# Attention-times-values with the values as weights in four column tiles, in a two-layer transformer kernel on one core

## The chip, the core and the metric

The kernel runs on one core of one Trainium2 chip. Five engines work side by side: TensorE (PE: matrix products, with its weight loads, PEld, shown apart), VectorE (DVE), ScalarE (ACT), GpSimd (POOL) and SyncE (SP, which here only issues DMAs). They wait for each other through semaphores. The metric is device time in microseconds (us), the median of three runs.

## The reference, cut to what matters

The reference is a chain of four residual blocks over x of 8 batches x 100 rows x 512. The change touches the third, a quantized cross-attention with 16 heads of 32:

```python
x = x + _L0_xattn_ref(_layernorm(x), ctx, ...)
x = x + _L0_ffn_ref(_layernorm(x), ...)
x = x + _L1_xattn_ref(_layernorm(x), ctx, mask, wq, bq, wk, bk, wv, bv, wo, bo)
x = x + _L1_ffn_ref(_layernorm(x), ...)

# _L1_xattn_ref, in words: q = w8a8(x), k, v = linear(ctx)      (361 context rows)
# p = softmax(q k^T / sqrt(32) + mask)                          (100 x 361 per head)
# o = p v                                                       (100 x 32 per head)
# out = w8a8(o, wo) + bo      (o is quantized by its row: max, scale, round)
```

The core of the change is `o = p v` and the division of the softmax by its row sums.

## The kernel before, in words

The program has three stages. Stage A (up to about 300 us) makes the first two blocks and, for each batch, the keys (into `CT`) and the values (into `VS`). Stage B (about 300 to 618 us) is the attention. Stage C is the mixture of experts. All fp32 matmuls appear in the trace as two instructions each (two passes of weights); the products on `float32r` tiles (scores) and the turns (transposes) are one instruction each.

Stage B takes the eight batches one after another (`batches`, a first batch, a loop of three times two, a last one), each with 16 steps, one per head. Every engine's order is written out by hand in its own `body`; the step number is `h_`. At a step,

- PE makes the scores of head `h_` (L793, `ps` bank 0 or 1), turns the exponentials of head `h_ - 2` in three pieces of 121 context rows (L802, `TURN = 2`), and multiplies head `h_ - 3` with the values (L814, `MIX = 3`): the turned exponentials `pT` (121 x 100) are the weights, and 33 columns of `VS` are streamed, 32 values and a column of ones whose product is the row sum. Three pieces are added up in a part of bank 4 or 5.
- DVE adds the mask, negates, and takes the row minimum (L1174).
- ACT makes the exponential (L612) and copies the turned exponentials of head `h_ - 2` out of PSUM (L621).

Two buffers of each (`score`, `masked`, `exp`, `p_turned`, `p_copied`, indexed by `h_ % 2`) let the engines run at most two heads apart. Around the heads lie, at fixed steps, the works of the next batch (on DVE `prep_at`: norm, quantization and bias of the queries; on PE the turn of `xq2b` at step 5 and `queries` at step 7; on ACT `high_keys` at step 5; on POOL `low_keys`) and of the batch before (on DVE `finish_at`: `finish1` divides by the row sums at step 2, `finish2` adds a bias at 5, `finish3` finds the scale at 6, `finish4` rounds at 7, `finish5` at 13; on PE the turn of `oQb` at step 9 and `out_rows`, L783, at step 11). SP's queue restacks keys and queries for the next batch (L335): for each quarter of the heads it waits until the scores of the current batch have read it; the third quarter's keys go ahead of the queries of the first quarter. It also loads expert weights, the second half after `o_norm` (`finish1`).

Of the kernel before, what the change touches and what calls it, by code (L numbers as in the profile page):

```python
# [5 lines left out]
ALU = mybir.AluOpType  # L6
# [9 lines left out]
T = 361  # L16
P = 128
# [6 lines left out]
VW = HEADS * (HD + 1)  # L24
# [14 lines left out]
def block_kernel(nc, x, ctxT, mask, decay, win, b_in, wout, b_out, gamma0, beta0, w1, w2, gammaf,  # L39
                 wq, bq, wk, bk, wv, bv, wo, bo, gate_w, gate_b, gate_bias, ew1, eb1, ew2, out):  # L40
    with ExitStack() as whole:
# [5 lines left out]
        def sem(name):  # L47
            if name not in sems:
# [6 lines left out]
                    "o_norm", "summ_used", "t1", "t2", "v_copied", "v_mm", "x1", "x2", "x3", "y_out0", "y_out1",  # L55
                    *(f"{name}{r}" for name in ("exp", "masked", "p_copied", "p_turned", "pv", "score")
# [77 lines left out]
        pT = sb(bb, "pT", [P, 2, NT, S])  # L134
# [107 lines left out]
        TURN, MIX = 2, 3  # L242
# [150 lines left out]
        def _(g):  # L393
# [45 lines left out]
            def body(b, last):  # L439

                alone(g, ("h_round", b + 1), ("t2", after(b * 2)))
                g.tensor_scalar(hq[0:S, FF // 2:], h[0:S, FF // 2:], -MAGIC, 1.0, ALU.add, ALU.mult)\
                 .then_inc(sem("hq1"), 1)
                if not last:
                    norms(b + 1)

                g.wait_ge(sem("v_copied"), after((b + 1) * NT))
                g.tensor_copy(vs(b)[0:TC, :].rearrange("p (c h w) -> p c h w", c=NT, h=HEADS)[:, :, :, HD],
                              ones[0:TC, 0:NT * HEADS].rearrange("p (c h) -> p c h", c=NT))\
                 .then_inc(sem("v_ones"), 1)  # L450

# [4 lines left out]
            g.wait_ge(sem("v_ones"), B)  # L456
# [64 lines left out]
        def _(act):  # L521
# [84 lines left out]
            def body(b, j, u, first, last):  # L606
                for h_ in range(HEADS + (TURN if last else 0)):
                    if h_ < HEADS:
                        r, n = h_ % 2, b * 8 + h_ // 2
                        act.wait_ge(sem(f"masked{r}"), after(n + 1))  # L610
                        act.wait_ge(sem(f"p_turned{r}"), after(n))
                        act.activation(pE[0:S, r, 0:T], sN[0:S, r, 0:T], ACT.Exp, scale=-1.0,  # L612
                                       bias=nmx[0:S, h_:h_ + 1]).then_inc(sem(f"exp{r}"), 1)
                    at_turn = behind(b, h_ - TURN, first)
                    if at_turn:

                        bt, ht = at_turn
# [3 lines left out]
                        act.copy(pT[0:TC, r].rearrange("p c s -> p (c s)"), ps[0:TC, 2 + r, 0:NT * S])\  # L621
# [5 lines left out]
                    if h_ == 10 and not first:  # L627
                        turned_o(b - 1)

# [3 lines left out]
            batches(act, body)  # L633
            turned_o(B - 1)
# [28 lines left out]
        def _(pe):  # L663
            for name in credited:
                pe.sem_inc(sem(name), 1)
            pe.wait_ge(sem("consts"), 1)
# [118 lines left out]

            def body(b, j, u, first, last):
                for h_ in range(HEADS + (MIX if last else 0)):
# [18 lines left out]
                    if at_mix:  # L806
                        bm, hh = at_mix
                        r, n, hd = hh % 2, bm * 8 + hh // 2, head(hh)[2]
                        pe.wait_ge(sem(f"p_copied{r}"), after(n + 1))
                        if hh == 0:  # L810
                            pe.wait_ge(sem("o_norm"), after(bm))
# [15 lines left out]
                    if h_ == 9 and not first:  # L827
# [4 lines left out]
                    if h_ == 11 and not first:  # L832
# [7 lines left out]
            batches(pe, body)  # L840
# [70 lines left out]
        def _(dve):  # L911
# [113 lines left out]
            def body(b, last):  # L1025
# [22 lines left out]
                for c in range(NT):  # L1048
                    if c == NT - 1 and not last:
                        rows(b + 1)  # L1050
                    dve.wait_ge(sem("v_mm"), after(b * NT + c + 1))
                    dve.tensor_copy(vs(b)[0:TC, c * VW:(c + 1) * VW].rearrange("p (h w) -> p h w", h=HEADS)[:, :, 0:HD],
                                    ps[0:TC, c % 2, :].rearrange("p (h w) -> p h w", h=HEADS))\
                       .then_inc(sem("v_copied"), 1)
# [83 lines left out]
            def finish1(b):  # L1138
                chf.turn(b)
                for r in range(2):  # L1140
                    dve.wait_ge(sem(f"pv{r}"), after((b + 1) * 8))
                o = ps[0:S, 4:6, 0:8 * (HD + 1)].rearrange("p g (h w) -> p g h w", h=8)
                chf(dve.reciprocal(rinv[0:S].rearrange("p (g h) -> p g h", g=2), o[:, :, :, HD]))
                dve.tensor_tensor(oN[0:S].rearrange("p (g h w) -> p g h w", g=2, h=8), o[:, :, :, 0:HD],
                                  rinv[0:S].rearrange("p (g h) -> p g h", g=2).unsqueeze(3)
                                  .to_broadcast([S, 2, 8, HD]), ALU.mult).then_inc(sem("o_norm"), 1)

            def finish2(b):
# [3 lines left out]
            def finish3(b):  # L1152
                row_scale(chf, oN[0:S], tb[0:S, 6:7], tb[0:S, 7:8], tb[0:S, 8:9])

            def finish4(b):
# [3 lines left out]
            def finish5(b):  # L1159
# [7 lines left out]
            def body(b, j, u, first, last):  # L1167
                dve.wait_ge(sem(f"mask_in{j}"), 16 * u + 16)
                for h_ in range(HEADS + 1):
# [7 lines left out]
                    if not first and h_ in finish_at:  # L1177
                        finish_at[h_](b - 1)
# [6 lines left out]
            finish_at = {2: finish1, 5: finish2, 6: finish3, 7: finish4, 13: finish5}  # L1185
# [10 lines left out]
            for step in finish_at.values():  # L1196
                step(B - 1)
# [152 lines left out]
```

## Time and profile before

| | us |
|---|---|
| median of 3 runs (lowest to highest) | 867.86 (866.38 to 868.89) |
| span of the profiled execution | 862.6 |
| what the median has beyond that span (start and end around it) | 5.3 |
| PE busy / PE weight loads busy | 632.2 / 511.1 |
| DVE / ACT / POOL busy | 411.9 / 295.8 / 139.9 |
| six batches of stage B, from the first score of the second batch (369.54) to that of the eighth (574.79) | 205.25 |

The span is from the first to the last instruction. Busy time is a union, so a weight load that lies under a product counts in both PE rows. "Granted clock" is the share of 2.4 GHz that TensorE had; it has two levels, 0.5 (1.2 GHz) and 1.0 (2.4 GHz). A batch's pitch is the time from its first score product to that of the next batch.

### The profile page before, as it was taken

The numbers are of one execution on the slowest core, as the hardware profiler recorded it, in microseconds if no ns is written. First come the engines' busy times: TensorE is split into PE (matmuls) and PEld (weight loads), VectorE is DVE, ScalarE is ACT, GpSimd is POOL, SyncE is SP. The second block draws the span as 40 slices with busy tenths as digits, with TensorE's granted clock in tenths as the row PEclk, the third lists the DMA queues.
The fourth block names the chain that finished last, engine by engine and source line by source line (L and its number), as shares of the span: only waits on it lengthen the run. The fifth ranks groups of instructions, "written<-read, shape, count | busy, mean of one in ns | idle before, by whom it ended". The sixth has DMA issues, their size and how long they took to land.

```text
span 862.6 us, 11350 instructions
## 1 busy us (share of the span) xinstructions
PE 632.2 (73%) x3228; PEld 511.1 (59%) x3229; DVE 411.9 (48%) x972; ACT 295.8 (34%) x503; POOL 139.9 (16%) x179
## 2 busy tenths in 40 slices
PE   0145599999999813999999999999327059999920
PEld 0124377777777512998998989989227035555510
DVE  6466467666667454464655656644241112111114
ACT  4166233344443241544453444544101012222210
POOL 1001133222133001210111101200000600000044
PEclk9985699999999955555555555555555579999975
DMA  8968000000000126537446465471300422222135
GB/s 350 370 238 262 10 10 9 9 9 0 9 9 1 32 87 134 108 109 169 113 121 143 114 148 122 115 165 68 88 14 0 126 87 85 85 85 85 61 83 169
DMA packets 57158, 86.42 MB, mean 100 GB/s; under 512 B 19858, under 2 KB 43186, under 8 KB 55114
## 3 DMA queue, kind: packets, MB, share of 16 engines
q1 hardware_dynamic: 54062, 79.57, 31.4%
q0 software_dynamic: 3072, 6.56, 2.8%
q8 instruction: 11, 0.18, 0.1%
q14 instruction: 13, 0.11, 0.0%
HBM read 47.88 MB, written 15.42 MB: 73 GB/s over the span
## 4 chain that ended last, share of the span: by engine, by line
PE 43%; DVE 5%; issue 4%; DMA 4%; POOL 3%; ACT 2%; SPq 1%; POOLq 0%; DVEq 0%; ACTq 0%
PE ps L814 12%; PE ps L802 7%; PE ps L901 7%; PE ps L887 6%; PE ps L793 5%; DMA b1B<-in_eb 1%; PE ps L783 1%; POOL picked L515 1%; PE ps L776 1%; POOL slots_in L508 1%; PE ps L861 1%; ACT hTe L648 1%; DMA q<-qH 1%; PE ps L893 1%; PE ps L855 1%
## 5 line engine op out<-in xcount | busy, mean ns | idle before, releaser
L814 PEld LDWEIGHTS ps<-VS,pT 121*100 121x100 f32 x768 | 132.7, 268 | 14.6 <-issue 12.3
L814 PE MATMUL ps<-VS,pT 121*100 (+1 forms) x768 | 134.6, 329 | 9.1 <-ACT pT L621 6.5
L612 ACT ACTIVATE pE<-sN,nmx 100x361 f32<-100x361 f32 x128 | 76.4, 598 | 145.4 <-DVE nmx L1174 145.3
L1174 DVE CUSTOM_DVE_ANT_0 sN<-ps,maskS 100x361 f32<-100x361 f32 x128 | 68.3, 534 | 107.6 <-PE ps L793 104.1
L802 PEld LDWEIGHTS ps<-ident,pE 100*121 100x121 f32 x384 | 97.4, 299 | 1.7 <-ACT pE L612 0.8
L802 PE MATMUL ps<-ident,pE 100*121 100x100 f32 x384 | 92.6, 374 | 0.0
L793 PE MATMUL ps<-K,q 96*100 96x364 f32 x128 | 74.6, 585 | 7.6 <-DMA q<-qH 7.1
L901 PE MATMUL ps<-VS,hTe 118*128 x120 | 56.7, 609 | 5.4 <-ACT hTe L648 5.4
L1274 DVE TENSOR_TENSOR hb<-ps,b1B 128x352 f32<-128x352 f32 x20 | 10.5, 524 | 96.8 <-PE ps L887 96.8
L887 PE MATMUL ps<-CT,xT 128*128 x160 | 52.6, 472 | 2.1 <-DVE xT L1268 2.1
L621 ACT COPY pT<-ps 121x300 f32<-121x300 f32 x128 | 49.7, 389 | 0.8 <-PE ps L802 0.8
L887 PEld LDWEIGHTS ps<-CT,xT 128*128 128x128 f32 x160 | 31.1, 196 | 24.9 <-issue 12.8
L465 POOL TENSOR_TENSOR CT<-CT,KH 128x1456 f32 (+1 forms) x8 | 26.2, 3273 | 93.9 <-ACT KH L594 93.9
L515 POOL DMA_INDIRECT picked<-slots_out,slotI x16 | 18.0, 1124 | 143.1 <-issue 143.1
L793 PEld LDWEIGHTS ps<-K,q 96*100 96x100 f32 x128 | 34.1, 267 | 10.2 <-DMA q<-qH 6.7
L1034 DVE TENSOR_REDUCE tk<-h 100x1 f32<-100x512 f32 x32 | 20.0, 679 | 39.6 <-ACT h L566 39.5
L901 PEld LDWEIGHTS ps<-VS,hTe 118*128 118x128 f32 x120 | 21.1, 189 | 29.2 <-issue 29.2
L697 PE MATMUL ps<-cxH,wkH 128*128 128x364 f32 x128 | 31.2, 369 | 8.8 <-DVE cxL L972 4.5
L677 PE MATMUL ps<-kvw,w1s 128*128 128x8 f32 x32 | 7.0, 361 | 39.8 <-DMA y<-in_b_out 39.8
L879 PE MATMUL ps<-ident,xin 128*128 128x128 f32 x80 | 12.5, 280 | 29.6 <-DMA xin<-slots_in 29.6
L697 PEld LDWEIGHTS ps<-cxH,wkH 128*128 128x128 f32 x128 | 22.7, 206 | 14.2 <-issue 7.1
L559 ACT ACTIVATE CT<-ps,biases 128x364 f32 (+1 forms) x32 | 17.9, 564 | 36.5 <-PE ps L697 35.6
(229 smaller groups left out, 1116.6 us busy)
## 6 DMA issues: line engine op xcount, KB each, us to landing
K<-KH SPq DMA_DIRECT2D x64, 182.0 KB, 3.8
VS<-in_w SPq DMA_DIRECT2D x8, 1024.0 KB, 8.9
CT<-in_ctxT SPq DMA_DIRECT2D x8, 728.0 KB, 16.4
K<-CT SPq DMA_DIRECT2D x32, 182.0 KB, 6.8
VS<-in_ew SPq DMA_DIRECT2D x8, 708.0 KB
CT<-in_ew SPq DMA_DIRECT2D x8, 704.0 KB
slots_in<-zeros SPq DMA_DIRECT2D x5, 1024.0 KB, 9.2
xin<-slots_in SPq DMA_DIRECT2D x20, 256.0 KB, 2.6
```

Source lines behind the costliest of these rows:

```text
L465: g.tensor_tensor(CT[:, b, :].bitcast(F32R), CT[:, b, :], KH[:].rearrange("p k t -> p (k t)").bitcast(F32), ALU.subtract)\
L515: g.indirect_dma_start(picked[0:S, k, b, :], None, slots_out, bass.IndirectOffsetOnAxis(slotI[0:S, k, b:b + 1], 0), bounds_check=NBLK * P ...
L612: act.activation(pE[0:S, r, 0:T], sN[0:S, r, 0:T], ACT.Exp, scale=-1.0, bias=nmx[0:S, h_:h_ + 1]).then_inc(sem(f"exp{r}"), 1)
L621: act.copy(pT[0:TC, r].rearrange("p c s -> p (c s)"), ps[0:TC, 2 + r, 0:NT * S])\
L697: mm = pe.matmul(ps[:, m % 2, 0:TP], wt[:, k, m * P:(m + 1) * P], cx[:, k, :], start=(n == 0), stop=(n == 3 * KC - 1))
L793: pe.matmul(ps[0:S, r, 0:TP], q3[:, hd, :], K3[:, hd, :], start=True, stop=True)\
L802: mm = pe.transpose(ps[0:TC, 2 + r, c * S:(c + 1) * S], pE[0:S, r, c * TC:(c + 1) * TC], ident[0:S, 0:S])
L814: mm = pe.matmul(ps[0:S, 4 + hd // 8, hd % 8 * (HD + 1):(hd % 8 + 1) * (HD + 1)], pT[0:TC, r, c, :], vs(bm)[0:TC, at:at + HD + 1], start=( ...
L887: mm = pe.matmul(ps[:, 2 + j, 0:EH], xT[:, j, k, :], CT[:, e, k * EH:(k + 1) * EH], start=(k == 0), stop=(k == KC - 1))
L901: mm = pe.matmul(ps[:, 7 - j, :], hTe[0:EC, 1 - j, c, :], vs(e)[0:EC, c * D:(c + 1) * D], start=(c == 0), stop=(c == 2))
L1034: ins = dve.tensor_reduce(tk[0:S, 14 + m:15 + m], h[0:S, m * 512:(m + 1) * 512], AX.X, ALU.max, apply_absolute_value=True)
L1174: dve.tensor_tensor_reduce(out=sN[0:S, r, 0:T], in0=ps[0:S, r, 0:T], in1=maskS[0:S, j, 0:T], scale=-1.0, scalar=3.4e38, op0=ALU.add, op1=A ...
```

## The change

The two operands of `p v` change places. The weights are now 32 columns of the values, the turned exponentials are streamed (100 columns), and the result is 32 rows (the head's columns) x 100. Four heads that lie 32 columns apart in the four 128-column chunks (`k * HPC + g`) write to four groups of 32 partitions of bank 4, so their weights sit in four column tiles of the array. One group of 12 products follows every fourth head (`MIX = 4`, `mix_group`). The column of ones is gone from `VS` (and POOL's fill of it); the row sums come from the exponential's accumulator on ACT (`accum_out`). The result lies the wrong way round, so ACT copies it (`rows_out`, step 4), PE turns it back in four transposes (`rows_back`, step 5), and DVE divides (`finish1`, now at step 6). The other finish steps move to 7, 8, 9 and 15, the turn of `oQb` to 11, `out_rows` to 13, ACT's `turned_o` to 12. `pT` has eight buffers in place of two. PE's `body` is written out for all eight batches, without a loop.

```diff
-VW = HEADS * (HD + 1)
+VW = HEADS * HD
-        pT = sb(bb, "pT", [P, 2, NT, S])
+        pT = sb(bb, "pT", [P, 2 * KC, NT, S])
+        sums, oTs = sb(bb, "sums", [P, 2, HEADS]), sb(bb, "oTs", [P, HPC, S])
-        TURN, MIX = 2, 3
+        TURN, MIX = 2, 4
@@ ACT
-                        act.activation(pE[0:S, r, 0:T], sN[0:S, r, 0:T], ACT.Exp, scale=-1.0,
-                                       bias=nmx[0:S, h_:h_ + 1]).then_inc(sem(f"exp{r}"), 1)
+                        act.activation(pE[0:S, r, 0:T], sN[0:S, r, 0:T], ACT.Exp, scale=-1.0, bias=nmx[0:S, h_:h_ + 1],
+                                       accum_out=sums[0:S, j, h_:h_ + 1]).then_inc(sem(f"exp{r}"), 1)
...
-                        act.wait_ge(sem(f"pv{r}"), after(n))
+                        act.wait_ge(sem("mixed"), groups_mixed(bt * HPC + ht // KC - 1))
...
+                    if h_ == 4 and not first:
+                        rows_out(b - 1)
...
+            def rows_out(b):
+                act.wait_ge(sem("mixed"), groups_mixed((b + 1) * HPC))
+                act.wait_ge(sem("o_back"), after(b))
+                act.copy(oTs[:].rearrange("p r s -> p (r s)"), ps[:, 4, 0:HPC * S]).then_inc(sem("oT_out"), 1)
@@ PE
+            def mix_group(b, g):
+                for r in range(2):
+                    pe.wait_ge(sem(f"p_copied{r}"), after(b * 8 + 2 * g + 2))
+                if g == 0:
+                    pe.wait_ge(sem("oT_out"), after(b))
+                for c in range(NT):
+                    for k in range(KC):
+                        hd = k * HPC + g
+                        at = c * VW + hd * HD
+                        mm = pe.matmul(ps[k * HD:(k + 1) * HD, 4, g * S:(g + 1) * S], vs(b)[0:TC, at:at + HD],
+                                       pT[0:TC, (g * KC + k) % (2 * KC), c, :], start=(c == 0), stop=(c == NT - 1))
+                mm.then_inc(sem("mixed"), 1)
+            def rows_back(b):
+                pe.wait_ge(sem("oT_out"), after(b + 1))
+                pe.wait_ge(sem("o_norm"), after(b))
+                for g in range(HPC):
+                    mm = pe.transpose(ps[0:S, 5, g * P:(g + 1) * P], oTs[:, g, :], ident[:, :])
+                mm.then_inc(sem("o_back"), 1)
...
-                        for c in range(NT):
-                            at = c * VW + hd * (HD + 1)
-                            mm = pe.matmul(ps[0:S, 4 + hd // 8, hd % 8 * (HD + 1):(hd % 8 + 1) * (HD + 1)],
-                                           pT[0:TC, r, c, :], vs(bm)[0:TC, at:at + HD + 1],
-                                           start=(c == 0), stop=(c == NT - 1))
-                        mm.then_inc(sem(f"pv{r}"), 1)
+                    if at_mix and at_mix[1] % KC == KC - 1:
+                        mix_group(at_mix[0], at_mix[1] // KC)
+                    if h_ == 5 and not first:
+                        rows_back(b - 1)
@@ DVE
+                dve.wait_ge(sem("o_back"), after(b + 1))
+                chf(dve.reciprocal(rinv[0:S], sums[0:S, j]))
...
-            finish_at = {2: finish1, 5: finish2, 6: finish3, 7: finish4, 13: finish5}
+            finish_at = {6: finish1, 7: finish2, 8: finish3, 9: finish4, 15: finish5}
```

PE, one step of a head in the second batch, before (`ps<-VS,pT` is the product with the values; an ISA row sets registers for it):

```order
L793 MATMUL ps<-K,q 100x364
L802 MATMUL ps<-ident,pE 121x100 x3
L814 ISA
L814 MATMUL ps<-VS,pT 100x33
L814 ISA
L814 MATMUL ps<-VS,pT 100x33
L814 ISA
L814 MATMUL ps<-VS,pT 100x33
```

PE, the steps 5 to 8 of the second batch, now (line numbers of the changed kernel: L823 scores, L832 turns, L805 values, L813 the result turned back):

```order
L823 MATMUL ps<-K,q 100x364
L832 MATMUL ps<-ident,pE 121x100 x3
L813 MATMUL ps<-ident,oTs 100x128 x4
L776 MATMUL ps<-identb,xq2b 128x100 x4
L823 MATMUL ps<-K,q 100x364
L832 MATMUL ps<-ident,pE 121x100 x3
L823 MATMUL ps<-K,q 100x364
L832 MATMUL ps<-ident,pE 121x100 x3
L805 MATMUL ps<-pT,VS 32x100 x12
L782 MATMUL ps<-ident,tb 128x100
```

Three products of 100 x 33 behind every head have become twelve of 32 x 100 behind every fourth, with nothing of another head between them, and four transposes stand ahead of the turn of `xq2b`.

DVE, the steps 7 and 8 of the second batch, before (L1174 is the mask step of a head, `oN` the batch before's result, `qt` the next batch's queries):

```order
L1174 ISA sN,nmx<-ps,maskS 100x361
L1174 ISA nmx 100x1
L1156 TENSOR_SCALAR oN<-oN,tb 100x512
L231 REGISTER_ALU
L1157 TENSOR_SCALAR oQb<-oN 100x512
L263 REGISTER_ALU
L1174 ISA sN,nmx<-ps,maskS 100x361
L1174 ISA nmx 100x1
L1123 COPY sxB<-ps 128x100
L231 REGISTER_ALU
L1124 TENSOR_TENSOR qt<-ps,sxB 128x400
```

DVE, from the end of step 8 to the end of step 9, now (L1196 is the mask step):

```order
L1146 TENSOR_TENSOR qt<-ps,sxB 128x400
L232 REGISTER_ALU
L1196 ISA sN,nmx<-ps,maskS 100x361
L1196 ISA nmx 100x1
L1178 TENSOR_SCALAR oN<-oN,tb 100x512
L232 REGISTER_ALU
L1179 TENSOR_SCALAR oQb<-oN 100x512
L1150 TENSOR_TENSOR qt<-qt,swqB 128x400
L232 REGISTER_ALU
L1151 TENSOR_TENSOR qt<-qt,bqB 128x400
L232 REGISTER_ALU
L268 REGISTER_ALU
```

The rounding of the result (`finish4`) has moved from a step of its own to behind the queries' rescaling, and shares its step with their bias.

## Rows read from the trace of the kernel before

**Rows 1.** The page: span, busy times, and granted clock in 40 slices.
```profile
span 862.6 us, 11350 instructions
PEclk9985699999999955555555555555555579999975
```

**Rows 2.** Windows: first and last full batch of stage B, and sum over six.
```profile
core 0: us, PE busy (x) PEld busy (x) DVE busy (x) ACT busy (x) POOL busy (x), PEclk, DMA share, GB/s
369.54:403.87 34.33, 32.78 (x192) 31.33 (x191) 20.52 (x57) 16.66 (x37) 5.35 (x4) 0.55 0.53 132
...
540.77:574.79 34.02, 32.76 (x191) 31.06 (x191) 20.50 (x57) 16.25 (x35) 5.35 (x4) 0.55 0.54 132
sum 205.25, PE 196.78 PEld 187.04 DVE 123.02 ACT 98.05 POOL 32.04; mean PE 32.80 PEld 31.17 DVE 20.50 ACT 16.34 POOL 5.34
```

**Rows 3.** Timeline: one head's steps (start us, us, engine, line, operation).
```profile
439.87 0.29 PEld L793 LDWEIGHTS ps<-K,q 96*100 96x100 f32 x1
...
440.75 1.13 PEld L814 LDWEIGHTS ps<-VS,pT 121*100 121x100 f32 x6
...
441.75 0.29 PEld L793 LDWEIGHTS ps<-K,q 96*100 96x100 f32 x1
441.82 0.61 PE L793 MATMUL ps<-K,q 96*100 96x364 f32 x1
...
442.64 0.54 DVE L1174 CUSTOM_DVE_ANT_0 sN<-ps,maskS 100x361 f32<-100x361 f32 x1 [1.34 <-PE ps L793]
...
443.22 0.60 ACT L612 ACTIVATE pE<-sN,nmx 100x361 f32<-100x361 f32 x1 [0.99 <-DVE nmx L1174]
```

**Rows 4.** Waits in stage B: who waited for whom, us in total, times, longest.
```profile
DVE sN L1174 <- PE ps L793: 104.1, 104, 4.2
```

**Rows 5.** The line L814: ns min/median/max, first and last start.
```profile
L814 PE MATMUL ps<-VS,pT x768: 195/355/377, 344.1 to 608.2; 121*100 x144, 121*100 121x33 f32 x48
```

**Rows 6.** The chain in stage C: eight fp32 passes of 352 columns at clock 1.0.
```profile
711.28 2.37 PE ps L887 x8
```

**Rows 7.** Timeline: four fp32 passes of 512 columns over 8-column weights.
```profile
50.49 1.92 PE L683 MATMUL ps<-w2s,xm 128*8 128x512 f32 x4
```

**Rows 8.** Timeline, stage C at clock 1.0: four fp32 turns of 128 columns.
```profile
703.14 0.60 PE L879 MATMUL ps<-ident,xin 128*128 128x128 f32 x4
```

**Rows 9.** Timeline: ACT's accumulator read, and its copy of 128 x 400.
```profile
69.09 0.19 ACT L540 ACTIVATION_READ_ACCUMULATOR hq<-VS 128x1 f32 x1
...
613.10 0.49 ACT L603 COPY oQT<-ps 128x400 bf16<-128x400 bf16 x1 [5.79 <-PE ps L767]
```

**Rows 10.** Timeline: finish4's first operation and POOL's low_keys; the former alone.
```profile
452.09 3.27 POOL L465 TENSOR_TENSOR CT<-CT,KH 128x1456 f32 x1 [10.60 <-ACT KH L594]
453.60 2.04 DVE L1156 TENSOR_SCALAR oN<-oN,tb 100x512 f32<-100x512 f32 x1
...
611.54 0.49 DVE L1156 TENSOR_SCALAR oN<-oN,tb 100x512 f32<-100x512 f32 x1
```

**Rows 11.** DVE by line in one batch: operations that share steps now.
```profile
L1101 DVE TENSOR_REDUCE tb<-oN 100x1 f32<-100x512 f32 x1 | 0.7, 682 | 0.0
...
L1129 DVE TENSOR_TENSOR qt<-qt,bqB 128x400 f32<-128x400 f32 x1 | 0.6, 575 | 0.0
```

**Rows 12.** The chain at a batch's end: the queries' DMA, then the scores.
```profile
466.31 6.63 DMA q<-qH
...
473.06 0.62 PE ps L793
```

**Rows 13.** Windows around the products of L783 (532.35 us): granted clock, third from last.
```profile
531.84:535.25 3.41, 3.41 (x16) 2.62 (x15) 0.46 (x3) 0.89 (x2) 0.00 (x0) 0.50 0.79 179
535.25:538.66 3.41, 3.11 (x28) 2.79 (x27) 2.42 (x8) 1.78 (x4) 0.25 (x1) 1.00 0.45 110
538.66:542.07 3.41, 2.90 (x17) 2.66 (x15) 1.05 (x6) 1.70 (x4) 1.01 (x1) 0.50 0.50 112
```

More of the change, by code:

```diff
@@ L54, in block_kernel @@
         credited = ("g1", "g2", "gelu", "hq0", "hq1", "hqT0", "k_copied", "oQT", "oQb",
-                    "o_norm", "summ_used", "t1", "t2", "v_copied", "v_mm", "x1", "x2", "x3", "y_out0", "y_out1",
-                    *(f"{name}{r}" for name in ("exp", "masked", "p_copied", "p_turned", "pv", "score")
+                    "o_norm", "o_back", "oT_out", "summ_used", "t1", "t2", "v_copied", "v_mm", "x1", "x2", "x3", "y_out0", "y_out1",
+                    *(f"{name}{r}" for name in ("exp", "masked", "p_copied", "p_turned", "score")
                       for r in range(2)))
@@ L239, in head, with groups_mixed @@
             return i % KC, i // KC, i % KC * HPC + i // KC
-        TURN, MIX = 2, 3
+        TURN, MIX = 2, 4
+        def groups_mixed(groups):
+            return groups + 2
         def behind(b, i, first):
@@ L445, in body @@
                     norms(b + 1)
[L447 to L450, printed above, removed]
             g.wait_ge(sem("vec_in"), 64)
@@ L626, in body @@
                         turned_x(b + 1)
-                    if h_ == 10 and not first:
+                    if h_ == 12 and not first:
                         turned_o(b - 1)
+            def rows_out(b):
+                act.wait_ge(sem("mixed"), groups_mixed((b + 1) * HPC))
+                act.wait_ge(sem("o_back"), after(b))
+                act.copy(oTs[:].rearrange("p r s -> p (r s)"), ps[:, 4, 0:HPC * S]).then_inc(sem("oT_out"), 1)
             act.wait_ge(sem("wq_t"), 8)
@@ L826, in body @@
                         queries(b + 1)
-                    if h_ == 9 and not first:
+                    if h_ == 11 and not first:
                         if not last:
@@ L831, in body @@
                         turn_rows(oQb, "oq_t", b - 1)
-                    if h_ == 11 and not first:
+                    if h_ == 13 and not first:
                         if not last:
@@ L839, in _ @@
             queries(0)
-            batches(pe, body)
+            for b in range(B):
+                body(b, b % 2, b // 2, b == 0, b == B - 1)
+            rows_back(B - 1)
             pe.wait_ge(sem("oQb"), after(B))
@@ L1136, in prep_split, with finish1, finish2, finish3 @@
                 chp.end()
-            def finish1(b):
+            def finish1(b, j):
                 chf.turn(b)
[L1140 to L1148, printed above, removed]
+                dve.wait_ge(sem("o_back"), after(b + 1))
+                chf(dve.reciprocal(rinv[0:S], sums[0:S, j]))
+                dve.tensor_tensor(oN[0:S].rearrange("p (k r w) -> p r k w", k=KC, r=HPC),
+                                  ps[0:S, 5, :].rearrange("p (r k w) -> p r k w", r=HPC, k=KC),
+                                  rinv[0:S].rearrange("p (r k) -> p r k", r=HPC).unsqueeze(3)
+                                  .to_broadcast([S, HPC, KC, HD]), ALU.mult).then_inc(sem("o_norm"), 1)
+            def finish2(b, j):
                 dve.wait_ge(sem("o_norm"), after(b + 1))
                 chf(dve.tensor_tensor(oN[0:S], oN[0:S], bvB[0:S], ALU.add))
-            def finish3(b):
+            def finish3(b, j):
                 row_scale(chf, oN[0:S], tb[0:S, 6:7], tb[0:S, 7:8], tb[0:S, 8:9])
-            def finish4(b):
+            def finish4(b, j):
                 chf(dve.tensor_scalar(oN[0:S], oN[0:S], tb[0:S, 8:9], MAGIC, ALU.mult, ALU.add))
                 dve.tensor_scalar(oQb[0:S], oN[0:S], MAGIC, None, ALU.subtract).then_inc(sem("oQb"), 1)
-            def finish5(b):
+            def finish5(b, j):
                 dve.wait_ge(sem("wo_mm"), b + 1)
@@ L1196, in _ @@
             for step in finish_at.values():
-                step(B - 1)
+                step(B - 1, (B - 1) % 2)
             dve.wait_ge(sem("x3"), after(B))
```

17 lines of the change are left out of this document (5 added, 12 removed).

## The prediction

> **What bounds the kernel now.** The page comes first, for the clock. Of its 40 slices, those from about 300 to 690 us stand at half clock [rows 1]; that is stage B and the start of stage C. The windows come next, cut at the first score of each batch. Six batches take 205.25 us, a pitch of 34.2, and in it PE is busy 32.8, DVE 20.5, ACT 16.3, POOL 5.3 [rows 2]. So TensorE bounds stage B. The waits say the same from the other side: DVE's mask step waited 104 us in 104 waits for the scores [rows 4]. The timeline of one head then shows what TensorE does. From the weight load of one head's scores to that of the next are 1.88 us (439.87 to 441.75). The first 0.88 (to 440.75) are scores and turns, the last 1.00 are the six weight loads of the product with the values [rows 3]. They follow each other every 0.167 us, though their products stream 33 columns only; each of them reads 355 ns from start to end, so the products overlap, and the loads of 100 columns are the bound [rows 5]. In a batch that is 16 x 0.88 = 14.1 for scores and turns, 16 x 1.00 = 16.0 for the values, and 34.2 - 30.1 = 4.1 for queries, output rows and turns of rows. The clock rises once in a batch, to 1.0 behind the products of L783, and falls again at 538.66 [rows 13]; the 4.1 is therefore net of what that stretch gives back.
>
> **What goes and what comes, part by part.** The 16.0 us of weight loads go. In their place stand 4 groups of 12 products, 24 passes each. A load now has 32 columns, an estimate of 0.167 x 32/100 = 0.053 us. A pass streams 100 fp32 columns: eight passes of 352 take 2.37 at full clock, 0.84 ns a column, so 0.084 us for 100, and 0.168 at half clock [rows 6]. That weights of few columns don't shorten a pass is in the four of 512 over 8-column weights: 1.92, or 0.48 each with the last one's tail, near 512 x 0.84 ns = 0.43 [rows 7]. So the price hangs on how many passes run at once in the four column tiles, and no row of before shows two at once. The bounds are: none at once, 24 x 0.168 = 4.0 a group, 16.1 a batch, what goes comes back; all four tiles at once, 6 x 0.168 = 1.0 a group, but 24 loads x 0.053 = 1.3, so 5.1 a batch. I take a value between. The two passes of one product use the same tile and follow each other, as before (768 instructions for 384 products [rows 5]), so the second waits for the first; only the next product's first pass can go beside it. That makes 13 slots instead of 24, 13 x 0.168 = 2.2 a group, 8.7 a batch.
>
> The Trainium skill ("TensorE: Matmul & The Clock Gate", Part 3, measured speedup) has three column tiles at 2.38 times one after another. By that rule the batch would pay 16.1/2.38 = 6.8 for the values, an estimate from its figure. No run here shows it.
>
> Each group is entered and left through a change from whole-array to column-tile products, eight changes a batch. If the array has to empty at each, the end of one product is paid that the next one covers now: 0.355 - 0.167 = 0.19 us [rows 5], 1.5 a batch. If not, nothing. I take 1.5, since nothing in the trace shows a change that is free. The Trainium skill ("TensorEngine Tiling (Array Packing)", Key Properties) speaks against this change here: it says that changing the tiling mode drains TensorE. The trace of before doesn't test it; with the rule the 1.5 stays, without it the pitch is 1.5 shorter.
>
> The way back: four transposes. Four fp32 turns of 128 columns take 0.60 at full clock with their tail [rows 8]; at half clock I take 0.8 a batch (bounds 0.6 and 1.2). ACT's copy of 128 x 400 takes 0.49 [rows 9]. It stands at step 4 behind the exponential of head 4 and the copy of head 2, and PE waits for it at step 5, with `xq2b`'s turn, all later scores and so DVE's masks queued behind. From the start of a head's scores to the start of its exponential are 443.22 - 441.82 = 1.4 us, and the exponential takes 0.6 [rows 3]; then come 0.39 for the copy of head 2 and 0.49, so `oTs` is there 2.9 us after the scores of head 4. PE has by then done two heads without values, 1.76. It waits 1.1 us. The accumulator read lengthens each exponential by about 0.1 (0.19, of which half lies under the end of the ACTIVATE) [rows 9]: 1.6 a batch on ACT, which is busy 16.3 of 34.2 and hides it; it delays a turn only where PE already waits.
>
> DVE is the next limit. It loses nothing and gains nothing in its sum, but `finish3` now shares step 8 with the queries' rescaling and `finish4` step 9 with their bias. `finish4` read 2.04 us while POOL ran `low_keys`, and 0.49 alone [rows 10]; two steps later it should be clear of POOL, so I count 0.49. From the scores of head 8: mask until 1.3, reduce 0.68 and its two small operations, copy and rescale 0.57 until 3.1; mask until 3.8; round twice 0.95 and two queries' operations of 0.57 until 5.9 [rows 11]. PE wants head 11's scores at 3 x 0.88 = 2.6 and needs mask 9, at 3.8; the turn of head 9 waits a little more. I take 1.3 us a batch. If POOL still overlaps, 1.5 more.
>
> The keys' and queries' DMAs are covered now by little: in one batch the queries landed 472.94, the scores started 473.06 [rows 12]. The piece from head 11 to the next batch holds five heads, two groups of values and the output rows in place of five heads with their values, about as long as before. So they stay hidden at 1.2 GHz. At a faster TensorE they are the floor there, with DVE.
>
> The sum for a batch, clock as before: 34.2 - 16.0 + 8.7 + 1.5 + 0.8 + 1.1 + 1.3 = 31.6, a gain of 2.6. POOL's fill of ones and PE's register instructions were beside other work and give nothing. At the end of stage B the way is longer: one whole group after the last copy (2.2 against two heads' 2.0), ACT 0.49, transposes 0.8, two hand-overs of about 0.2: 1.9. Eight batches give 20.8 - 1.9 = 19, against the span of 862.6: 844; with the 5.3 us that the median has beyond the span, 849.
>
> **The clock.** The one rise in a batch stands behind the densest products of stage B, L783, and the stretches at 1.0 on the page are those of stage A and C, where fp32 streams of 352 and more columns follow each other [rows 1, 6, 13]. The values' products were loads with 33 columns of stream; now they are streams of 100 columns back to back, 2.2 us in every 5.7. I think it likelier than not that the clock rises more often. At 1.0 throughout, TensorE would fall below DVE: its 20.5 busy, some 45 gaps of 0.04 between dependent operations, and the two stalls of 1.1 and 1.3, an estimate of 24.7. Halfway between 31.6 and 24.7 is 28.2: 8 x 6.0 - 1.9 = 46 less, 822.
>
> **The rivals.**
> A, two tiles at once and the clock up about half of the time: 822, by the sum above. For it speaks the density; against it, that a column tile fills a quarter of the array, and that the clock fell at once when it had risen [rows 13].
> B, two at once and the clock as now: 849.
> C, four at once, clock as now: 31.6 - 8.7 + 5.1 = 28.0 a batch, 868 - 50 + 2 = 820. Against it the pairs in one tile.
> D, nothing at once, but the clock up half of the time: 34.2 + 0.1 + 1.5 + 0.8 + 1.1 = 37.7 at half clock, 24.7 again where DVE rules; halfway 31.2, 8 x 3.0 - 4 = 20 less, 848.
> E, the other side: nothing at once, clock as now. The place is the group of 24 passes, its price 4.0 against the 4.0 of loads that it replaces, so that the changes, the way back and the wait for `oTs` are all added: 37.7, 3.5 more a batch, 28, and 4 at the end (the last group is 4.0): 900; without the 1.5 for the changes, 888. It decides from 11.3 a batch for the values on (16.0 less the 4.7 that is added), that is from 17 slots a group.
> F, about the same: the overlap is there, but loads of a tile don't go beside a product of the same tile, and each slot gets 0.053 and a hand-over longer; 13 x 0.06 x 4 = 3 eats the gain: 868.
>
> **How the numbers follow.** A 0.37, B 0.22, C 0.12, D 0.09, E 0.15, F 0.05. The forecast is A's time, 822; C would come out at nearly the same. The range reaches from 798 (a pitch of 25.2, nearly DVE's floor) to 874 and leaves out E and a little below. A's own range is 800 to 845. About 0.3% is what a measurement of this kernel can tell from no change; A to D are faster by more, and F splits: faster 0.80, same 0.05, slower 0.15.
>
> **What would show it.** In the windows, a pitch of 26 to 30. In the timeline of a group, starts of passes in twos, 2.2 us from the first to the next score at half clock; single file at 0.168 would be D or E, and fours would be C. More than one stretch at 1.0 a batch says A, one says B. PE idle about 1.1 us ahead of the transposes with ACT's copy as the releaser; DVE's `finish4` at 0.49; mask steps no longer waiting for scores at steps 8 to 10, but scores for masks. A queries' DMA ahead of each batch's first score says that the floor there is reached. The forecast is wrong if a group takes over 2.8 us of TensorE at half clock, or if the pitch is over 33.

## The result: 887.9 us, slower, and the profile after

The changed kernel takes 887.86 us (884.59 to 890.04, four runs) against 867.12 (861.97 to 868.89) for the kernel before in the same comparison: a ratio of 1.0256, 95% interval 1.0223 to 1.0289. The forecast was 822, its range 798 to 874.

The page of the changed kernel: span, busy times, granted clock in 40 slices, and two lines (busy us, mean ns | idle before them and what ended most of it).

```profile
span 884.9 us, 11236 instructions
PE 576.5 (65%) x3260; PEld 425.7 (48%) x3261; DVE 410.8 (46%) x972; ACT 307.6 (35%) x639; POOL 138.5 (16%) x171
PEclk9975799999999755555665555555655559999975
...
L823 PE MATMUL ps<-K,q 96*100 96x364 f32 x128 | 75.6, 592 | 71.5 <-DMA q<-qH 63.9
...
L805 PE MATMUL ps<-pT,VS 121*32 121x100 f32 x768 | 36.9, 357 | 0.6 <-ACT pT L620 0.6
```

The span grew by 22.3 while PE's busy time fell from 632 to 576.5. So TensorE has less to do and stands idle more, and the line of the scores says for what: 63.9 us for the queries' DMA. The windows from the first score of a batch to that of the next, the third batch shown, and then all six full ones together:

```profile
core 0: us, PE busy (x) PEld busy (x) DVE busy (x) ACT busy (x) POOL busy (x), PEclk, DMA share, GB/s
403.35:442.43 39.08, 25.71 (x194) 20.65 (x194) 20.43 (x57) 17.71 (x52) 5.33 (x4) 0.59 0.48 120
...
364.27:601.35 237.08, 154.18 (x1159) 122.06 (x1159) 122.39 (x342) 106.24 (x312) 31.98 (x24) 0.56 0.46 115
```

Against [rows 2] the pitch is 39.5 in place of 34.2, and PE is busy 25.7 of it in place of 32.8. DVE and POOL do what they did; ACT does 1.4 more (17.7 in place of 16.3). The waits of stage B (who for whom, us in total, times, longest):

```profile
DVE sN L1196 <- PE ps L823: 130.8, 58, 10.2
...
PE ps L823 <- DMA q<-qH: 63.9, 8, 9.9
...
PEld ps L813 <- ACT oTs L635: 8.0, 8, 1.0
```

DVE's mask still waits for scores, as in [rows 4], in fewer waits (58 in place of 104) that sum up to more (130.8 us in place of 104.1) and last up to 10.2 us: at the start of each of the last six batches it waits over 9 us for the first score.

Where in a batch the time lies is told by the starts of the score products (mean of the third to the sixth batch, us; S4 is the score of head 4). The columns e1 and e9 belong to experiments below.

| piece | before | after | e1 | e9 |
|---|---|---|---|---|
| S0 to S4 | 8.19 | 6.11 | 6.11 | 5.96 |
| S4 to S8 | 9.51 | 8.68 | 8.75 | 8.53 |
| S8 to S11 | 5.94 | 4.09 | 4.03 | 4.17 |
| S11 to S15 | 7.97 | 9.02 | 9.02 | 9.02 |
| S15 to the next S0 | 2.61 | 11.69 | 5.54 | 2.12 |
| pitch, mean of six | 34.21 | 39.51 | 33.72 | 29.95 |

The change took 4.8 us out of the first three pieces, gave back 1.0 in the fourth, into which the turn of `oQb` has moved out of the third, and lost 9.1 in the last. That piece takes 2.1 when nothing is late (e9); the rest is the wait for queries. Six times 5.3 is 31.8 more. The first batch, whose successor's keys and queries don't share the queue with expert loads, became 4.3 shorter (29.7 to 25.4). The last is 4.7 shorter up to its last score, since no queries follow that it could wait for, and the first score of all comes 1.0 earlier. So the last score of stage B stands at 625.45 against 603.63, 21.8 later: the whole of the span's 22.3 but for 0.5.

### The profile page after: what moved, and what is told of

The parts are those of the page before. It is cut to its first block, busy times and chain, and to the rows that moved or that the text cites. A ratio compares the mean times of both kernels' runs of the same rounds, so it can differ in the third digit from the quotient of the medians.

```text
span 884.9 us, 11236 instructions
## 1 busy us (share of the span) xinstructions
PE 576.5 (65%) x3260; PEld 425.7 (48%) x3261; DVE 410.8 (46%) x972; ACT 307.6 (35%) x639; POOL 138.5 (16%) x171
## 3 DMA queue, kind: packets, MB, share of 16 engines
q1 hardware_dynamic: 54062, 79.57, 30.5%
## 4 chain that ended last, share of the span: by engine, by line
PE 23%; SPq 11%; DMA 9%; issue 8%; DVE 4%; POOL 4%; ACT 3%; POOLq 0%; DVEq 0%; ACTq 0%
SPq L340 11%; PE ps L925 6%; DMA q<-qH 6%; PE ps L911 6%; PE ps L832 2%; PE ps L823 2%; PE ps L805 2%; DMA b1B<-in_eb 1%; POOL picked L514 1%; POOL slots_in L507 1%; PE ps L885 1%; POOL CT L464 1%; ACT hTe L656 1%; PE ps L917 1%; PE ps L879 1%
## 5 line engine op out<-in xcount | busy, mean ns | idle before, releaser
L1196 DVE CUSTOM_DVE_ANT_0 sN<-ps,maskS 100x361 f32<-100x361 f32 x128 | 67.3, 533 | 137.9 <-PE ps L823 130.8
L823 PE MATMUL ps<-K,q 96*100 96x364 f32 x128 | 75.6, 592 | 71.5 <-DMA q<-qH 63.9
L832 PE MATMUL ps<-ident,pE 100*121 100x100 f32 x384 | 98.6, 390 | 14.7 <-ACT pT L620 13.4
L832 PEld LDWEIGHTS ps<-ident,pE 100*121 100x121 f32 x384 | 92.3, 298 | 31.0 <-ACT pE L611 28.6
L823 PEld LDWEIGHTS ps<-K,q 96*100 96x100 f32 x128 | 33.5, 263 | 80.5 <-DMA q<-qH 66.3
L911 PEld LDWEIGHTS ps<-CT,xT 128*128 128x128 f32 x160 | 31.3, 197 | 24.8 <-issue 12.6
L805 PE MATMUL ps<-pT,VS 121*32 121x100 f32 x768 | 36.9, 357 | 0.6 <-ACT pT L620 0.6
L903 PE MATMUL ps<-ident,xin 128*128 128x128 f32 x80 | 12.7, 284 | 29.7 <-DMA xin<-slots_in 29.7
L474 POOL TENSOR_TENSOR xbo<-XR,boB 100x512 f32<-100x512 f32 x8 | 10.1, 1266 | 132.6 <-DVE XR L1187 132.6
L664 ACT COPY yb<-ps 128x512 f32<-128x512 f32 x20 | 11.7, 585 | 52.3 <-PE ps L925 52.3
```

What stands on the lines that cost most here:

```text
L805: mm = pe.matmul(ps[k * HD:(k + 1) * HD, 4, g * S:(g + 1) * S], vs(b)[0:TC, at:at + HD], pT[0:TC, (g * KC + k) % (2 * KC), c, :], start=(c ...
L823: pe.matmul(ps[0:S, r, 0:TP], q3[:, hd, :], K3[:, hd, :], start=True, stop=True)\
L832: mm = pe.transpose(ps[0:TC, 2 + r, c * S:(c + 1) * S], pE[0:S, r, c * TC:(c + 1) * TC], ident[0:S, 0:S])
L911: mm = pe.matmul(ps[:, 2 + j, 0:EH], xT[:, j, k, :], CT[:, e, k * EH:(k + 1) * EH], start=(k == 0), stop=(k == KC - 1))
L1196: dve.tensor_tensor_reduce(out=sN[0:S, r, 0:T], in0=ps[0:S, r, 0:T], in1=maskS[0:S, j, 0:T], scale=-1.0, scalar=3.4e38, op0=ALU.add, op1=A ...
```

## Why the queries are late: SP's queue

SP, the idle engine that only issues DMAs, is the one to follow. Its timeline in one batch of the kernel before (start us, us, what):

```profile
407.08 0.37 SPq L325 DMA_DIRECT2D CT<-in_ew  x1
410.99 0.25 SPq L327 DMA_DIRECT2D VS<-in_ew  x1
411.42 0.29 SPq L330 DMA_DIRECT2D maskS<-in_mask  x1
421.33 1.25 SPq L335 DMA_DIRECT2D K<-KH  x2
...
423.51 1.60 SPq L335 DMA_DIRECT2D K<-KH  x2
...
428.19 1.23 SPq L335 DMA_DIRECT2D K<-KH  x2
...
430.79 1.77 SPq L335 DMA_DIRECT2D q<-qH  x1
```

and of the changed kernel, one batch later:

```profile
445.77 0.37 SPq L330 DMA_DIRECT2D CT<-in_ew  x1
455.06 0.26 SPq L332 DMA_DIRECT2D VS<-in_ew  x1
455.51 0.30 SPq L335 DMA_DIRECT2D maskS<-in_mask  x1
457.20 1.29 SPq L340 DMA_DIRECT2D K<-KH  x2
...
459.76 4.93 SPq L340 DMA_DIRECT2D K<-KH  x2
464.84 1.92 SPq L340 DMA_DIRECT2D K<-CT  x1
466.92 2.90 SPq L340 DMA_DIRECT2D K<-KH  x2
469.96 0.62 SPq L340 DMA_DIRECT2D K<-CT  x1
470.62 0.64 SPq L340 DMA_DIRECT2D q<-qH  x1
```

In both the second expert load waits for `o_norm`, and the waits of SP's queue (whole of stage B; before, then after) show how long:

```profile
SPq L327 <- DVE oN L1144: 19.3, 7, 4.2
```

```profile
SPq L332 <- DVE oN L1165: 58.6, 7, 11.4
```

`o_norm` is `finish1`, and the change moved `finish1` from step 2 to step 6. Before, the load is issued 7.1 us after the first score (403.87) and has 10 us, but for the small mask, to itself before the keys are restacked at 421.33. After, it is issued 12.6 us after the first score (442.43), with the mask behind it, and 2.1 us ahead of the restack. The restack itself is not held up by it: it waits for POOL's `low_keys` and starts 14.8 us after the batch's first score in the changed kernel as in e1 below, where the load goes 6 us earlier. So the load costs time through the DMA engines that it shares with the restack. Windows of the DMA engines, before:

```profile
core 0: us, PE busy (x) PEld busy (x) DVE busy (x) ACT busy (x) POOL busy (x), PEclk, DMA share, GB/s
408.00:412.00 4.00, 3.64 (x20) 3.40 (x20) 2.47 (x8) 0.93 (x3) 0.00 (x0) 0.50 0.54 183
412.00:416.50 4.50, 4.50 (x27) 4.41 (x27) 3.45 (x12) 2.78 (x7) 0.00 (x0) 0.50 0.19 68
416.50:421.50 5.00, 5.00 (x37) 4.98 (x37) 3.98 (x9) 3.36 (x6) 3.28 (x1) 0.50 0.14 56
421.50:426.50 5.00, 5.00 (x32) 5.00 (x30) 3.35 (x10) 1.78 (x4) 0.00 (x0) 0.50 0.76 165
```

and after:

```profile
450.00:455.00 5.00, 4.21 (x32) 3.72 (x34) 2.74 (x9) 4.56 (x12) 1.24 (x1) 0.50 0.00 0
455.00:460.00 5.00, 3.99 (x49) 3.26 (x41) 4.56 (x10) 2.31 (x7) 2.04 (x1) 0.83 0.44 105
460.00:465.00 5.00, 2.65 (x35) 1.50 (x33) 4.36 (x12) 1.96 (x6) 0.00 (x0) 0.85 0.51 129
```

Before, the last of the 708 KB runs out at 68 and 56 GB/s while nothing else is wanted, and the restack starts at 165 GB/s. After, the engines first stand at 0 GB/s, because SP waits, and then the load, the mask and the restack go together at 105 and 129. SP's issue of the second pair of keys reads 4.93 us in place of 1.60. From the issue of the first keys to the landing of the first quarter's queries are 24.7 us (457.20 to 481.9); in the kernel before they are 15.9 (421.33 to 437.22).

## Experiments

A ratio is to the kernel before, run on the same chip in the same comparison, with its 95% interval.

**e1: the load's wait back where it was.** The load goes into the batch's values, so it may go once the last values' product has read them.

```diff
-sp.wait_ge(sem("o_norm"), after(b + 1))
+sp.wait_ge(sem("mixed"), groups_mixed((b + 1) * HPC))
 sp.dma_start(vs(b)[0:EC, 0:3 * D], ew2[b])...
```

> The changed kernel, but SP's second expert load (708 KB into VS) waits for the last value product of its batch (mixed, PE's step 3) in place of the division (o_norm, DVE's step 6). Theory 'load': the loss comes from that load, which now goes to the DMA engines about 2 us ahead of the restack of keys and queries (455.06 against 457.20), so that the queries land 20 us behind head 11's scores in place of 9.6, and PE stands still 8 to 10 us at each batch. With the load some 7 us earlier the pitch falls from 39.6 to 29.5 to 31.5 us, and the time to 825 to 840. Rival 'restack': keys and queries take that long by themselves once TensorE is faster, whatever else is loaded; then PE waits at least 7 us a batch as now and the time stays within 875 to 890.

Measured: 851.33 us, 0.9834 (0.9804 to 0.9864), pitch 33.72. One line of SP's queue is worth 36 us and the sign of the change. But the size was not as expected (825 to 840): PE still waits for queries, half as long.

```profile
407.15 0.25 SPq L332 DMA_DIRECT2D VS<-in_ew  x1
...
415.50 1.25 SPq L340 DMA_DIRECT2D K<-KH  x2
...
423.19 0.58 SPq L340 DMA_DIRECT2D q<-qH  x1
```

```profile
PE ps L823 <- DMA q<-qH: 29.9, 8, 6.5
```

**e2: the same harm done to the kernel before.** Only the load's wait is moved later, to `oQb` (`finish4`).

```diff
-sp.wait_ge(sem("o_norm"), after(b + 1))
+sp.wait_ge(sem("oQb"), after(b + 1))
```

> The kernel before, with one wait changed: the second expert load waits for oQb (DVE's step 7) in place of o_norm (step 2). Nothing of the products changes. Theory 'load': this alone makes the queries late, by 6 to 10 us a batch over six or seven batches: 900 to 935 us, with PE's scores waiting for the queries' DMA. Rival 'restack': the load's place doesn't matter, 863 to 872.

Measured: 933.58 us, 1.0793 (1.0758 to 1.0827), pitch 44.91, of which 13.11 from S15 to the next S0 (2.61 before). That is at the upper end of what was expected. The load now goes 18.3 us after a batch's first score and 1.0 ahead of the restack, which itself starts 1.8 us later than before. PE waited for queries, the same wait at the same place, with no change to any product (six batches):

```profile
PE ps L793 <- DMA q<-qH: 64.5, 6, 11.7
```

**e3: the load still waits for `o_norm`, but behind the restack.**

```diff
-    sp.wait_ge(sem("o_norm"), after(b + 1))          # in expert_loads
-    sp.dma_start(vs(b)[0:EC, 0:3 * D], ew2[b])...
 ...
     stack_batch(it * 2 + j + 2, False)
+    second_half(it * 2 + j)                          # the same two lines
```

> The changed kernel, but the second expert load is issued behind the restack of keys and queries of its turn, and the mask's load ahead of it. Theory 'load': nothing large stands ahead of the restack, pitch 29 to 31.5, 825 to 842 us; a little may come back where the load now meets the fourth quarter's keys. Rival 'restack': 875 to 890.

Measured: 853.03 us, 0.9842 (0.9813 to 0.9871); pitch 32.33, shorter than e1's but longer than the 29 to 31.5 expected. It gives back what it gains over e1 at the start of stage C, where DVE waited 20.5 us for the bias `b1B`, whose DMA is queued behind the last loads (14.7 in the kernel before, at the same place, and 11.4 in e1).

**e4: do four column tiles run at once?** From e1, with the two loops of a group exchanged, so that the six passes of one tile follow each other.

```diff
-for c in range(NT):
-    for k in range(KC):
+for k in range(KC):
+    for c in range(NT):
```

> e1 with the two inner loops of mix_group exchanged: the three products of one column tile follow each other before the next tile's come. In the trace of the changed kernel four passes start within 0.02 us and the next four 0.167 later. Theory 'order': that hangs on neighbours in the stream being in different tiles; tile by tile the 24 passes go nearly in single file (only the last of a tile beside the first of the next), 21 x 0.168 = 3.5 us a group against 1.0, so 10 us more a batch: 905 to 925 us if e1 is at 832. Rival: the array looks ahead over tiles whatever the order, and the time is e1's within 5 us.

Measured: 859.0 us, 0.9927 (0.9898 to 0.9955), pitch 34.71. The group's timeline here:

```profile
407.17 2.23 PE L805 MATMUL ps<-pT,VS 121*32 121x100 f32 x24
409.33 0.62 PE L823 MATMUL ps<-K,q 96*100 96x364 f32 x1
```

and in the changed kernel, with the chunk outside:

```profile
446.55 0.90 PE L832 MATMUL ps<-ident,pE 100*121 100x100 f32 x3 [0.23 <-ACT pT L620]
447.38 1.23 PE L805 MATMUL ps<-pT,VS 121*32 121x100 f32 x24
448.54 0.62 PE L823 MATMUL ps<-K,q 96*100 96x364 f32 x1
```

Both expectations missed: tile by tile isn't single file (4.0), it is 2.2. Each tile starts 0.34 us, two passes, after the one before it (407.166, 407.507, 407.847, 408.187), so a tile's last four passes run beside the next tile's first four. The other order has 1.23. That settles the overlap. Four groups longer by 1.0 are 4.0 a batch, but the pitch rose by 1.0 only; the granted clock stood at 1.0 for 106 us of stage B where it was 44 in e1, which is where some of it went.

**e5: queries earlier in the restack.** From e1; the first two quarters' queries go ahead of the third quarter's keys, the third's right behind them.

```diff
-    if r == HPC - 1:
+    if r == HPC - 2:
         sp.wait_ge(sem("q_ready"), b + 1)
-        for q in range(HPC - 1):
+        for q in range(HPC - 2):
             stack(q3, (qH, qL, qH), q)
     ...
     stack(K3, (KH, KH, low), r)
-stack(q3, (qH, qL, qH), HPC - 1)
+    if r >= HPC - 2:
+        stack(q3, (qH, qL, qH), r)
```

> e1 (the second expert load waits for the last value product) and in the restack the queries of the first two quarters go ahead of the third quarter's keys in place of behind them. In e1 a batch's first score still waits some 4 us for the queries, which land 15.1 us behind head 11's scores, in a pitch of 33.7. Theory 'queue': they are late because three transfers of 182 KB stand ahead of them in the queue; moved up they land about 4 us earlier and the pitch falls to 29.5 to 31, the time to 820 to 836. Rival 'start': the keys' restack as a whole starts too late (415.5, 14.8 us behind the first score) and takes 19 us to the queries' landing; then the third quarter's keys become what the next batch waits for and at most 1 us a batch is won: 843 to 851.

Measured: 845.29 us, 0.9757 (0.9715 to 0.9799), pitch 32.41: the fastest version of the study, 22 us below the kernel before. That is less than was hoped for (820 to 836) and the rival's time. PE's wait for queries falls by a third. Over the six full batches alone:

```profile
PE ps L824 <- DMA q<-qH: 15.4, 6, 4.7
```

where e1 has 23.4 in the same stretch; with the wait for the very first queries it is 22.0 against the 29.9 above. The 8 us are the six pitches, 1.3 shorter each.

**e6, e7, e8, e11: high parts of the keys earlier on ACT**, so that the restack can start earlier: at step 3 on e1 (e6), on e5 (e7), on the kernel before together with e5's order (e8), and at step 4 on e5 (e11).

```diff
-if h_ == 5 and not last:
+if h_ == 3 and not last:
     high_keys(b + 1, False)
```

> e1 with ACT's high_keys at step 3 in place of step 5, so that POOL's low_keys and with it the restack start some 3 us earlier. Theory 'queue' alone: the third quarter's keys wait for head 11's scores as before and the queries stand behind them: no more than 1 us a batch, 843 to 851. Rival 'start': 2 to 3 us a batch, 828 to 838.

> Both edits of e5 and e6. By either theory the next batch no longer waits for the queries: a pitch of 29 to 30.5, the sum of what TensorE does and waits for inside a batch (S0 to head 11 in 18.8, from there to the end of the batch's last value group 10.7): 818 to 832 us.

> The kernel before (products as before) with the edits of e5 and e6. If these two alone were worth what e7 wins, the changed products would be worth nothing. TensorE bounds the kernel before with 32.8 us of 34.2, and its batches waited 0.6 us at most for the queries; so both theories expect 863 to 870, no gain. Rival: the restack's DMAs also hold the kernel before, 845 to 858.

> e5 (load at the last value product, first quarters' queries ahead) with high_keys at ACT's step 4, behind the copy of the result, in place of step 5. At step 3 (e6, e7) it held up ACT's copy of the result and ran POOL's low_keys beside DVE's rounding of the next queries. At step 4 both should be gone and the restack start 1 to 1.5 us earlier. Theory 'start': 833 to 841 us. Rival: the collision with DVE stays and eats it, 843 to 850.

Measured: e6 851.17, 0.9823 (0.9769 to 0.9877), against e1's 851.33; e7 851.98, 0.9823 (0.9773 to 0.9873); e11 847.14, 0.9772 (0.9739 to 0.9804), against e5's 845.29; e8 877.27, 1.0117 (1.0079 to 1.0155), 1.2% slower than before. None gained; e7 and e8 lie outside everything that was expected of them, e11 at its rival's time. In e6 the wait for queries did fall, from 29.9 us to 21.9, but S4 to S8 grew from 8.75 to 10.24: POOL's `low_keys` now runs beside DVE's rounding of the queries into `xq2b`, which reads 3.36 us in place of 0.43. In e8 it is `finish2` that reads 3.0. In e7 ACT waited for the restack of the batch before to have read the keys, and PE for ACT's copy:

```profile
PE ps L814 <- ACT oTs L636: 23.5, 8, 6.2
...
ACT KH L594 <- DMA q<-qH: 22.6, 7, 5.1
```

In e11 the restack starts 0.9 us earlier than in e5 (13.9 in place of 14.8 after the batch's first score) and nothing comes of it: the pitch is 32.56 against 32.41. An earlier start alone doesn't help; whether DMA time is what is missing, the next two runs tell.

**e9 and e10: no expert loads in stage B.** From e1 and from the kernel before; both loads of all batches are issued once stage B is over. Stage C then waits for 11 MB, so the total time is of no interest; the pitch is.

```diff
-    stacked(sp, b)                                   # in expert_loads
-    sp.dma_start(CT[:, b, 0:KC * EH], ew1[b])...
-    sp.wait_ge(sem("mixed"), ...)
-    sp.dma_start(vs(b)[0:EC, 0:3 * D], ew2[b])...
 ...
 sp.wait_ge(sem("b_done"), 4)
+for b in range(B):
+    # both loads of batch b
```

> e1 with both expert loads (1.4 MB a batch) taken out of the attention stage and issued in a row behind it. The whole program gets 30 to 60 us longer there, so only the pitch of the batches counts. In e1 it is 33.7, with 3 to 4 us in which the first score waits for the queries. Theory 'shared DMA': the restack (2.8 MB a batch) and the expert loads share the 16 engines, and without the loads the queries land in time: pitch 29 to 30.5. Rival 'restack alone': the wait stays over 2 us and the pitch over 32.

> The kernel before with the same edit as e9. Both theories: the pitch stays at 34.2 (33.5 to 34.3), since TensorE bounds it; the difference of e10's and e9's pitch is then what the changed products are worth when nothing is late, by the trace's own rows 4 to 5 us a batch. If it is under 2 us, the products themselves were not the gain.

Measured: e9 958.18 us and e10 989.99 (one run each; 31.8 apart). Six batches of stage B, e9 and then e10:

```profile
366.22:545.92 179.70, 150.81 (x1159) 118.79 (x1159) 121.76 (x341) 106.09 (x312) 30.84 (x23) 0.59 0.47 102
```

```profile
369.82:575.04 205.22, 198.14 (x1137) 188.75 (x1136) 123.06 (x342) 97.99 (x212) 32.00 (x24) 0.54 0.41 89
```

With the loads gone, the changed products have a pitch of 29.95 (29.6 to 30.5 in the six batches), and their queries land over 3 us before they are wanted. The kernel before has 34.20, as with the loads: in its six batches PE waited for queries once, 0.6 us. So the products are worth 4.25 us a batch, and the shared DMA engines eat 3.8 of it even in e1 (33.72). PE's busy time a batch fell by 7.9 (33.0 to 25.1) and its idle time rose by 3.6 (1.2 to 4.8).

**e12: one load ahead of the restack, one behind it.** From e5.

```diff
-    sp.wait_ge(sem("mixed"), groups_mixed((b + 1) * HPC))    # in expert_loads
-    sp.dma_start(vs(b)[0:EC, 0:3 * D], ew2[b])...
 ...
     stack_batch(it * 2 + j + 2, False)
+    second_half(it * 2 + j)                                  # the same two lines
```

> e5 (second expert load at the last value product, first quarters' queries ahead of the third quarter's keys) with, inside the loop, the second expert load issued behind the restack as in e3. With the loads out of the stage the pitch was 29.95 (e9), with both in ahead of the restack 32.4 (e5), with one behind it and the queries last 32.3 (e3). Theory 'shared DMA': both edits add up, pitch 30.5 to 31.5, 832 to 842 us. Rival: the volume of a batch is what counts, not its place, and the load behind the restack delays the next batch's keys instead: pitch 32 to 33, 843 to 850.

Measured: 859.91 us, 0.9926 (0.9899 to 0.9952); pitch 32.59 against e5's 32.41. The pitch is the rival's (32 to 33): between these two places it doesn't matter where the load stands. And as in e3 stage C starts later (DVE waited 24.3 us there for `b1B`, 11.4 in e5), which makes the time longer than either expectation.

## Why the prediction was wrong

**The step that failed** is the paragraph on the keys' and queries' DMAs, which ended in "So they stay hidden at 1.2 GHz". It compared the length of the last piece of a batch before and after, and took the landing of the queries as fixed. It never followed SP's queue past the moved `finish1`, though the second load's wait for `o_norm` stood in the code and the moves of the finish steps were counted for every other engine. Right behind that wait stand the mask and the restack of keys and queries, and the load's bytes now move on the same DMA engines as theirs. The load at 12.6 us after S0 in place of 6.4 (e1; 7.1 before, [rows 2] give its S0) cost 5.8 us a batch (e1 against after), 36 us in all. None of the rivals A to F had it; E had the sign, but for a price on TensorE that wasn't paid.

**A second part of the same step**: even with the wait put right, "hidden" fails. The queries landed 0.1 us ahead of the scores in [rows 12], the tightest of six batches; the others had 0.4 to 1.3. That is hardly cover; it says that the DMA engines were already the second bound of a batch. With 1.4 MB of expert weights and the restack in each batch no order of the queue that was tried came below a pitch of 32.3 (e3; e5 32.4, e12 32.6, e1 33.7), so the forecast's 28.2 and even 31.6 were not reached. e9 shows the price, 3.8 us a batch. The comparison that the paragraph made did hold: from S11 to the next S0 are 10.6 us before and 11.1 in e9. What it left out is the part of the batch ahead of S11, which became 4.8 us shorter while the restack could start only 2.7 us earlier (14.8 in place of 17.5).

**The other terms** held up, were too dear, or lacked one:

- Values, 8.7 plus 1.5 for the changes of mode. The passes of one group start in fours, four within 0.02 us (447.384 to 447.404), the next four 0.167 later (447.552). From the last turn's slot to the next score are 1.30 us, 5.2 a batch for both. Rival C (four at once) was right on this. That "the second waits for the first" held, the pair of passes of one product did follow each other; what failed is "only the next product's first pass can go beside it": the passes of all three other tiles went beside each of them. The loads of 32 columns were no bound at 0.053 each either: those of four tiles start within 0.02 us as well.
- The changes themselves cost about 0.13 going in (0.340 from the last turn's start to the group's, where turns follow each other by 0.204) and 0.14 coming out, some 1.1 a batch where 1.5 was taken. The Trainium skill ("TensorEngine Tiling (Array Packing)", Key Properties) says that changing the tiling mode drains TensorE. The trace agrees as far as these two gaps go; it doesn't show the array empty. By the other rule weighed, the Trainium skill's three tiles at 2.38 times ("TensorE: Matmul & The Clock Gate", Part 3), the values would have been 6.8, an estimate from its figure; the 24 passes took 1.02 us a group, 4.1 a batch, where single file would be 4.0 a group.
- The way back, 0.8, reads 1.09 with its last transpose's tail, and 0.89 from its first start to the next product's; the wait for `oTs`, 1.1, is 0.79:

```profile
451.40 1.09 PE L813 MATMUL ps<-ident,oTs 128*100 128x128 f32 x4 [0.79 <-ACT oTs L635]
```

- ACT's accumulator read is 0.19 as in [rows 9]. That ACT hides it isn't shown. PE waits for ACT's copies of the turned exponentials more than before, which the sum had at nothing: 2.3 us a batch in e9 against 0.8 in e10. How much of it the reads cause, and how much comes from a faster PE, no run splits. The whole of stage B, e9, then e10:

```profile
PE ps L829 <- ACT pT L617: 14.1, 31, 0.8
PE ps L820 <- DVE nmx L1193: 8.3, 11, 1.0
```

```profile
PE ps L811 <- ACT pT L618: 4.9, 10, 0.7
```

- DVE's stall, 1.3: PE's scores waited for masks 1.3 us a batch in e9, the second line above.
- `finish4` at 0.49 is right. But the slow instruction did not go away: POOL's `low_keys` now meets `finish2`, which no one had asked about. It reads 2.36 us where it had 0.69 before, as `finish4` had 2.04 in place of 0.49 [rows 10]:

```profile
453.76 3.27 POOL L464 TENSOR_TENSOR CT<-CT,KH 128x1456 f32 x1 [7.88 <-ACT KH L593]
```

```profile
455.23 2.36 DVE L1172 TENSOR_TENSOR oN<-oN,bvB 100x512 f32<-100x512 f32 x1
...
461.01 0.48 DVE L1178 TENSOR_SCALAR oN<-oN,tb 100x512 f32<-100x512 f32 x1
```

**The sum against e9**, where nothing is late: 31.6 at the clock of before, 28.2 with a clock up half of the time, and 29.95 measured. TensorE's price for the values was 5.0 too high (8.7 + 1.5 against 5.2). About 3.3 came back elsewhere: 1.5 of it is PE's longer wait for ACT's copies, 0.4 a wait for ACT ahead of the output rows; how the rest splits isn't measured. Had the queries been in time, the kernel would stand near 835, an estimate (867 less the 31.8 between e10 and e9), inside the range and between the forecast and B.

**The clock.** Time at 1.0 in stage B went from 27 us to 41, in e1 44: it rose, as the forecast said, but only by about an eighth of the way to half of stage B. In e4, where the groups are twice as long, it was 106 us; what raised it there no run separates.

## What to carry to other kernels

When a step of one engine is moved, list every wait on its semaphore, those of the engine that only issues DMAs first, and read what is queued behind that wait. A transfer that lands just ahead of its use is a bound next to the one you are removing, and a saving on the engine beyond it is worth little (0.5 of 4.25 us a batch in e1) until the transfer, its start and what shares the DMA engines with it are moved as well; moving the others' loads out of the stage (e9) tells in one run what the saving would be. Put repeated fp32 products into column tiles in an order that changes the tile with each product.

## What the runs showed of the hardware

- Four column tiles with 121 rows and 32 columns of fp32 weights ran fully at once: 24 passes of 100 columns in 1.02 us at clock 0.5, the time of six. In tile order the same 24 took 2.0 (e4), each tile starting 0.34 us behind the one before. Why it doesn't start sooner no run here shows.
- An issue on SP's queue read 0.6 us for one part of the restack, and 1.92 for one or 4.93 for two in the 10 us behind an expert load. That the load's bytes hold up the issue is argued, not shown.
- Three operations of DVE from and to SBUF, 100 x 512, were held up beside POOL's `low_keys`: 2.36 us in place of 0.69 (`finish2`), 2.04 in place of 0.49 (`finish4`, before), 3.36 in place of 0.43 (`xq2b`, e6). The three ended 0.6, 0.3 and 0.3 us behind the end of `low_keys` (457.59 after 457.03; 455.64 after 455.36; 412.60 after 412.32). The masks, which read PSUM, kept their 0.54 beside it. In e6 the meeting with `xq2b` goes with 1.5 us more in S4 to S8.
